# Streamed cross-attention on one core: who issues the query transfers, and what stands ahead of them

## The reference, cut to what matters

```python
q = split_heads(layernorm(x) @ Wq + bq)      # 16 heads of 16, 128 tokens
k = split_heads(ctx @ Wk + bk)               # 12544 keys
v = split_heads(ctx @ Wv + bv)
scores = einsum('bhqd,bhkd->bhqk', q, k) / sqrt(16)
x = x + merge_heads(softmax(scores) @ v) @ Wo + bo
```

## Time and profile before

| | |
|---|---|
| median of 3 runs | 3372.61 us (3367.91 to 3373.32) |
| the profiled execution | 3372.62 us, its span 3370.9 us |
| mean granted TensorE clock | 0.906 of full speed |
| TensorE matmul busy | 2945.2 us (87%) |
| VectorE busy | 1830.0 us (54%) |
| ScalarE busy | 1350.9 us (40%) |
| DMA | 393.95 MB, mean 117 GB/s |
| L0, L1, L2 begin (first transfer issued) | at 458.13, 984.76 and 1500.56 us |

### The profile page before, as it was taken

One profiled execution on the slowest core, in us unless ns is written; L12 is line 12 of the kernel. 1 busy time (PEld: TensorE's weight loads), 2 busy tenths in 40 slices (PEclk: granted clock), 3 DMA queues, 4 the chain that ended last, 5 costly groups with the idle time before them and its releaser, 6 DMA issues. The chain is left out here.

```text
span 3370.9 us, 66496 instructions
## 1 busy us (share of the span) xinstructions
PE 2945.2 (87%) x27158; PEld 2487.7 (74%) x27158; DVE 1830.0 (54%) x3246; ACT 1350.9 (40%) x2191; POOL 404.1 (12%) x571
## 2 busy tenths in 40 slices
PE   6999809998768999477999669999999999999978
PEld 6888706776564777463777455999999999999867
DVE  5555418774527775446776343555555555555524
ACT  4444305665003666123667120444444444444311
POOL 2443400000100000000000002220202020200000
PEclk9999958998787999686999685999999999999969
DMA  4898879882468883158884271100101010000016
GB/s 154 281 289 270 269 152 182 177 176 64 153 187 177 174 176 78 46 191 178 175 176 101 82 220 36 52 18 22 39 1 39 1 39 1 1 1 1 17 50 227
DMA packets 251093, 393.95 MB, mean 117 GB/s; under 512 B 45827, under 2 KB 214149, under 8 KB 250789
## 3 DMA queue, kind: packets, MB, share of 16 engines
q1 hardware_dynamic: 250791, 389.70, 45.3%
HBM read 289.45 MB, written 99.49 MB: 115 GB/s over the span
## 5 line engine op out<-in xcount | busy, mean ns | idle before, releaser
L712 DVE TENSOR_REDUCE L_xattn_tops<-psum 128x1 f32<-128x896 f32 x672 | 702.4, 1086 | 270.3 <-PE psum L564 269.1
L625 ACT ACTIVATE L_xattn_probs<-psum 128x512 f32<-128x512 f32 x1176 | 612.3, 600 | 518.2 <-PE psum L575 518.1
L1720 DVE TENSOR_TENSOR L_units_low<-psum,L_units_high 128x896 fp32r<-128x896 f32 x224 | 243.6, 1088 | 486.8 <-ACT L_units_high L1669 486.8
L564 PE MATMUL psum<-L_xattn_keys,L_xattn_q_stack 96*128 96x448 bf16 (+1 forms) x1344 | 395.2, 378 | 110.5 <-DMA L_xattn_q_stack<-query_parts 65.2
L1637 PE MATMUL psum<-wide_tokens,L_units_high 128*128 128x386 f32 x1568 | 456.5, 358 | 1.4 <-DVE L_units_low L1720 1.4
L575 PEld LDWEIGHTS psum<-L_xattn_q_stack,L_xattn_keys 99*128 99x128 bf16 (+1 forms) x4704 | 323.1, 98 | 144.4 <-issue 19.2
L575 PE MATMUL psum<-L_xattn_q_stack,L_xattn_keys 99*128 99x128 bf16 (+1 forms) x4704 | 394.2, 221 | 5.0 <-ACT L_xattn_probs L625 5.0
L1638 PE MATMUL psum<-wide_tokens,L_units_low 128*128 128x194 f32 x1568 | 395.1, 252 | 0.0
L588 PE MATMUL psum<-L_xattn_probs,L_xattn_values 128*17 128x128 f32 x9408 | 358.5, 277 | 0.2 <-issue 0.2
L1669 ACT CAST L_units_high<-psum 128x896 fp32r<-128x896 f32 x224 | 203.3, 908 | 363.7 <-PE psum L1625 363.7
L1661 ACT ACTIVATE L_units_raw<-L_units_raw,L_units_negmax 128x896 f32<-128x896 f32 x224 | 221.6, 1036 | 308.4 <-DVE L_units_negmax L1711 308.4
(11 more groups left out here) (436 smaller groups left out, 3990.6 us busy)
## 6 DMA issues: line engine op xcount, KB each, us to landing
key_parts<-proj_parts SPq DMA_DIRECT2D x84, 672.0 KB, 5.1
L_xattn_keys<-key_parts SPq DMA_DIRECT2D x144, 336.0 KB, 4.7
values_scratch<-proj_values SPq DMA_DIRECT2D x18, 1904.0 KB, 11.9
L_xattn_values<-values_scratch SPq DMA_DIRECT2D x144, 238.0 KB, 5.4
L_ffn_w<-in_L_ffn_W SPq DMA_DIRECT2D x32, 1024.0 KB, 6.8
L_xattn_keys<-key_parts SPq DMA_DIRECT2D x144, 224.0 KB, 5.0
L_xattn_keys<-key_parts SPq DMA_DIRECT2D x192, 112.0 KB, 5.1
L_ffn_w<-in_L_ffn_w SPq DMA_DIRECT2D x16, 1024.0 KB, 6.3
```

The lines of the kernel that those rows point to most:

```text
L564: last = pe.matmul(top_slot(n)[:, s, :], q_stack[0:P1, h, :], keys[0:P1, v % RING, key:key + WIN // 2], start=True, stop=True)
L625: act.activation(group_probs(k), score_bank(k), ACT.Exp).then_inc(sem("probs"), 1)
L712: dve.tensor_reduce(tops[:, h % 2, 2 * c + w:2 * c + w + 1], top_slot(n), AX.XY, ALU.max)\
L1720: dve.tensor_tensor(low[gr][:], turned_banks(gr), high[gr][:], ALU.subtract).then_inc(sem("low"), 1)
```

## The change

Setup also writes one row of ones to DRAM (`ones_row`, 12,544 bf16), and the ones rows of `keys` are read from there. `qparts` goes to DRAM in one transfer that ScalarE issues. The six stack transfers are split, three on ScalarE's queue and three on SyncE's. SyncE issues only head 0's first pair before them; it then waits for the stack and issues head 0's other fills. In L1 and L2 the ones rows follow head 0's fills, and TensorE waits for them ahead of the first `scores`. In L0 mask and ones rows come ahead of the first fill.

```diff
@@ setup
             sp.dma_start(g.x[:], a["x"].rearrange("b t d -> (b t) d")).then_inc(st.sem("x"), 16)
-            sp.wait_ge(st.sem("x"), 16)
+            sp.wait_ge(st.sem("ones_bf"), 1)
+            sp.dma_start(dram(g.ones_row, 0, [[128, NK // 128], [1, 128]]), g.ones_bf[0:NK // 128, :])\
+              .then_inc(st.sem("x"), 16)
+            sp.wait_ge(st.sem("x"), 32)
...
-            dve.memset(g.ones_bf[:], 1.0)
+            dve.memset(g.ones_bf[:], 1.0).then_inc(st.sem("ones_bf"), 1)
@@ streamed_cross_attention
+            def stack_rows(eng, at, copies, part):
+                src = dram(g.query_parts, part * D * T, [[T, HD], [HD * T, H], [1, T]])
+                eng.dma_start(q_stack[at * HD + part:(at + copies) * HD:copies, :, :], src)\
+                   .then_inc(sem("stack"), 16)
+
+            def ones_rows(eng):
+                eng.dma_start(keys[SEG:SEG + 3, :, :], dram(g.ones_row, 0, [[0, 3], [0, RING], [1, CH]]))\
+                   .then_inc(sem("key_rows"), 16)
@@ SyncE
-                sp.dma_start(keys[SEG:SEG + 3, :, :].rearrange("p s (n t) -> p (s n) t", t=128),
-                             g.ones_bf[0:3, :].unsqueeze(1).to_broadcast([3, RING * TPC, 128]))\
-                  .then_inc(sem("key_rows"), 16)
-                for j in range(len(PAIRS)):
-                    fill(0, j)
-                if masked:
                     sp.wait_ge(sem("drop"), 1)
                     sp.dma_start(dram(g.mask_row, 0, [[NK // 128, 128], [1, NK // 128]]), drop_bf[:])\
                       .then_inc(sem("mask"), 16)
                     sp.wait_ge(sem("mask"), 32)
+                if masked:
+                    ones_rows(sp)
                     for p in range(DEEP):
                         sp.dma_start(keys[SEG + 3:SEG + 4, p * NCH:p * NCH + NCH, :],
-                                     dram(g.mask_row, 0, [[NK, 1], [CH, NCH], [1, CH]])).then_inc(sem("key_rows"), 16)
-
-                sp.wait_ge(sem("qparts"), 1)
-                for part in range(3):
-                    sp.dma_start(dram(g.query_parts, part * D * T, [[T, 128], [128 * T, DG], [1, T]]),
-                                 qparts[:, part, :, :]).then_inc(sem("qparts_out"), 16)
-                sp.wait_ge(sem("qparts_out"), 48)
-                for at, copies in ((0, 3), (3, 2), (5, 1)):
-                    for part in range(copies):
...
-                if masked:
+                                     dram(g.mask_row, 0, [[NK, 1], [CH, NCH], [1, CH]])).then_inc(sem("mask_rows"), 16)
                     sp.wait_ge(sem("stack_zero"), 1)
                     sp.dma_start(q_stack[SEG + 3:SEG + 4, :, :],
                                  g.ones_bf[0:1, :].unsqueeze(1).to_broadcast([1, H, T]))\
                       .then_inc(sem("stack"), 16)
+                fill(0, 0)
+                sp.wait_ge(sem("qparts_out"), 16)
+                for part in range(3):
+                    stack_rows(sp, 0, 3, part)
+                sp.wait_ge(sem("stack"), STACK)
+                for j in range(1, len(PAIRS)):
+                    fill(0, j)
+                if not masked:
+                    ones_rows(sp)
                 for h in range(1, H):
@@ TensorE
                 pe.wait_ge(sem("stack"), STACK)
-                pe.wait_ge(sem("key_rows"), 16 * (1 + DEEP) if masked else 16)
+                if masked:
+                    pe.wait_ge(sem("key_rows"), 16)
+                    pe.wait_ge(sem("mask_rows"), 16 * DEEP)
...
                 def scores(k):
                     h = (k * GROUP + GROUP - 1) // (NCH * TPC)
                     pe.wait_ge(sem("shifted"), 4 * (h + 1))
+                    if k == 0:
+                        pe.wait_ge(sem("key_rows"), 16)
@@ ScalarE
+                act.wait_ge(sem("qparts"), 1)
+                act.dma_start(dram(g.query_parts, 0, [[T, 128], [D * T, 3], [128 * T, DG], [1, T]]), qparts[:])\
+                   .then_inc(sem("qparts_out"), 16)
+                act.wait_ge(sem("qparts_out"), 16)
+                for part in range(2):
+                    stack_rows(act, 3, 2, part)
+                stack_rows(act, 5, 1, 0)
```

More of the change, by code:

```diff
@@ L513, in _ @@
                     sp.wait_ge(sem("mask"), 32)
+                if masked:
+                    ones_rows(sp)
                     for p in range(DEEP):
                         sp.dma_start(keys[SEG + 3:SEG + 4, p * NCH:p * NCH + NCH, :],
-                                     dram(g.mask_row, 0, [[NK, 1], [CH, NCH], [1, CH]])).then_inc(sem("key_rows"), 16)
-                sp.wait_ge(sem("qparts"), 1)
-                for part in range(3):
-                    sp.dma_start(dram(g.query_parts, part * D * T, [[T, 128], [128 * T, DG], [1, T]]),
-                                 qparts[:, part, :, :]).then_inc(sem("qparts_out"), 16)
-                sp.wait_ge(sem("qparts_out"), 48)
-                for at, copies in ((0, 3), (3, 2), (5, 1)):
-                    for part in range(copies):
-                        src = dram(g.query_parts, part * D * T, [[T, HD], [HD * T, H], [1, T]])
-                        sp.dma_start(q_stack[at * HD + part:(at + copies) * HD:copies, :, :], src)\
-                          .then_inc(sem("stack"), 16)
-                if masked:
+                                     dram(g.mask_row, 0, [[NK, 1], [CH, NCH], [1, CH]])).then_inc(sem("mask_rows"), 16)
                     sp.wait_ge(sem("stack_zero"), 1)
@@ L2818, in build @@
         g.mask_row = nc.dram_tensor("mask_row", (1, NK), BF16, kind="Internal").ap()
+        g.ones_row = nc.dram_tensor("ones_row", (1, NK), BF16, kind="Internal").ap()
         g.acc, g.neg_all = sb("acc", [T, H, VW]), sb("neg_all", [T, H])
```

## The result

The changed kernel takes 3354.78 us (median of ten runs, 3349.4 to 3363.1), the kernel before 3373.56 us in ten runs beside it: ratio 0.9942, 95% interval 0.9930 to 0.9954. It is faster, by 18.8 us where I had forecast 39.2, and outside my range. The profiled execution (3360.93 us) lies 6.1 us above its own median; before's lay within 1 us of its median. So I compare by stage: from the first transfer of a stage to the first transfer of the output part behind it, L0, L1 and L2 last 367.6, 365.2 and 357.0 us against 370.3, 373.1 and 365.8, that is 2.7, 7.8 and 8.9 less, 19.4 in all.

What follows compares the result with a forecast made beforehand. No engine bounds the whole; the heads of L0, L1 and L2 wait for the query stack. Gains of 12.7 (L0) + 2 x 13.5 (L1, L2) - 0.5 (setup) = 39.2 us give 3333.4 us, range 3316 to 3350.

Steps and rivals of the forecast that it cites:

- the query chain: L1 and L2, query parts through stack transfers to first matmul: first matmul 22.7 us earlier, bounds 21.5 and 23.5.
- the late fills: L1 and L2 lead phase: fills issued after the stack come 3.1 us late at pair 1, 4.2 at head 1's pair 1.
- I take 5.0: L1 and L2: the ones transfer takes 5.0 us on three DMA engines (6.2 or 4.0), delaying every fill behind it.
- the old rate: The old ones transfer's 6.4 GB/s an engine; in L1 and L2 11.8 us for the ones, delay 16.0 in all.
- second rival: L0, L1 and L2: ones go in as slowly as before, 11.8 us, one row read repeatedly; 3354 us, chance 0.10.
- first matmul at 484: L0: query parts and stack follow ones, mask rows and first fill; first matmul at 484 against 500.90, 16.9 us earlier.
- its upper end: L0: first matmul at 490, if ScalarE's first transfer takes turns with ones, mask rows and fill on the laden engine.
- the loads catch up and nothing more is lost: Behind the first scores a pair is wanted only every 5.4 us, so late fills cost nothing further there.
- The clock: L0, L1 and L2: granted clock 0.50 (1.2 GHz) rises as long after first scores as before; otherwise some 1.5 us a stage.
- Setup: Start of the kernel: writing the row of ones after the load of x costs 0.5 us, between 0.2 and 1.
- The bounds of my single terms: Gains: L0 between 6 and 17 us, L1 and L2 each between 5.5 and 20.5; setup cost between 0.2 and 1.

Runs made afterwards that it cites:

- f2: The changed kernel with ScalarE's four query transfers issued by SyncE again, in the same order; ratio to the kernel before 0.9948.
- e5: The changed kernel with the ones rows written by GpSimd (one third) and ScalarE (two thirds) at idle times, not by a transfer; ratio to before 0.9864.
- e2: The changed kernel with the ones rows sent as three transfers of one partition each; ratio to the kernel before 0.9949.
- e1: The changed kernel with the ones read from 63 different DRAM rows instead of one row read 63 times; ratio to the kernel before 0.9939.
- h3: The changed kernel, ones still by DMA, with head 2's pairs 1 to 3 and the fills of later heads held back; ratio to before 0.9923.
- h1: The kernel before, old order, with ones written by engines and the fills from head 2's pair 1 on held back; ratio to before 0.9873.
- g1: As e5, with head 2's pairs 1 to 3 paced and fills of head 3 and later waiting three chunks longer; ratio to before 0.9826.

## Why the prediction was wrong

**Right: the query chain.** I had L1's first matmul 22.7 us earlier; it came 23.2 earlier, 23.1 in L2. ScalarE's one issue took 0.40 us (I had 0.9), landed after 2.3 as assumed, and three issues on two queues and their landing took 4.4 (4.3). The rule that a second issuer saves only issue time held: 1 us (f2), half of the 1.9 I had given it.

**Right: the late fills.** I had 3.1 us at pair 1 and 1.1 behind it, 4.2. Without the ones (e5) the lead phase grew from 22.2 to 25.9 us in L1, 3.7, and to 27.7 in L2, 5.5.

**Wrong: the ones rows, "I take 5.0".** I had 9.2 us of delay for ones and fills together; measured are 14.0 and 14.4. The term was about 10 us; I had put it between 4.0 and 6.2, and at 11.8 only with the old rate. I priced the transfer by what DMA engines read and move, by how many it uses, and did not ask into which partitions it writes. The 6.4 GB/s an engine of the old transfer was read as an effect of its 256-byte pieces; for the three together it was 19 GB/s, close to the 22 that the new one shows with pieces fourteen times as long, and in e2 the ones had more engines and the wait fell by only 2 us. My second rival, with the old rate kept, named 3354 us and a wait of over 10 us, and both came. Its reason, one row read again and again, did not (e1), and it charged L0 6.8 us for the ones alone; the coincidence of the totals proves nothing. Cost: 4.8 and 5.2 us in L1 and L2.

**Wrong: L0, "first matmul at 484".** It came 11.5 us earlier, not 16.9. The forecast let the query parts pass beside ones and mask; its upper end, ScalarE's transfer taking turns with all of this, is what happened (16.0 us instead of 2.3, and 6.5 to 8.1 without the ones). Cost: 5.4 us.

**Wrong: "the loads catch up and nothing more is lost".** The loads did catch up, and that was the trouble. While they did, the DMA engines were full, and TensorE lost 5.4 us in L0 and 1.3 in L1, nothing in L2. Spreading the fills gave 5.6 and 2.0 of it back (h3), and nothing in the old order (h1). In e5, where the ones no longer held TensorE back, the same loss was 5.1 us in L1. That full engines go ahead of the loss is shown by these runs; by the timing of all 51 pieces, what TensorE then lacks is its next load of instructions; that rests on the coincidence in time, and no run tests it.

**The clock** was taken to rise as long after the first scores as before, with some 1.5 us a stage either way. It rose 2.5, 1.3 and 4.7 us sooner. So the losses behind the scores are larger than their net of 6.7 us, and that L2 shows none is luck.

**Setup** cost 0.1 us, not 0.5: the projection's first weight load is issued at 3.89, before at 3.79:

```profile
1.28 0.46 SPq L160 DMA_DIRECT2D ones_row<-ones_bf  x1
3.89 0.37 SPq L259 DMA_DIRECT2D proj_w_a<-in_L_xattn_Wk  x1
```

The sum by the steps: 39.2 forecast, less 5.4 (L0's first matmul), 10.0 (ones in L1 and L2) and 6.7 (behind the scores), plus 2.0 (0.9 for the first matmuls of L1 and L2, 0.7 for L0's lead phase, 0.4 for setup) are 19.1; measured are 18.8. They agree that well partly by chance: the stages were compared in one execution of each kernel, and by them the gain is 19.4. The bounds of my single terms, added up (6 + 2 x 5.5 - 1), reach down to a gain of 16 us, 3356.6; I had drawn the range narrower.

## What to carry to other kernels

A transfer into few partitions can be bound by those partitions' way into SBUF (here 22 to 27 GB/s), and the fills behind it wait with it; constant rows are better written by an engine that is idle just then. When work is moved forward, look at what its transfers now meet: a queue of prefetches that nothing holds back catches up at full share and can cost the consumer more than it brings, so give prefetches a due time. Here both together turn a ratio of 0.994 into 0.983 (g1) with the same order of the query chain.

## What was unexpected in the hardware

Judged by the wait that they cause, three rows of 75 thousand bytes on partitions 96 to 98 move at 22 GB/s, and at 27 in e2, where they land with seven signals each and not three in all; a load of the same kind on partitions 96, 104 and 112 causes a little over half the wait (4.0 us against 7.1). Behind 10 us with DMA shares of 1.03 and more, TensorE has idle pieces of 1.0 to 4.3 us that no semaphore explains (50 of 51), and every one ends 1.3 to 1.8 us behind a 16 KB packet of instructions. GpSimd's memset of 3 x 12,544 elements takes 10.6 us, and a VectorE cast of 0.29 us beside it takes 6.6 to 10.1. ScalarE's copy of the same size takes 10.6 us too.
